# Two-layer attention and gate stack on one core: odd heads' probabilities of the last two items and the last gate products on VectorE, spare products in the drain, negated mean ahead of the power

## What is computed

```
x = x + attn_a(layernorm(x))   # softmax attention with rotary terms
x = x + ffn(layernorm(x))
x = x + attn_b(layernorm(x))   # causal sparsemax attention
x = x + ffn(layernorm(x))

attn_*: 16 heads of 8 columns, scores 256 x 256 for each head
sparsemax(z) = max(z - tau, 0), tau from the sorted, summed scores
ffn(x) = (silu(x @ wg.T) * (x @ wu.T)) @ wd.T, hidden width 384
```

## Time and profile before

| | before |
|---|---|
| median of 3 runs | 621.91 us (621.61 to 622.36) |
| the profiled execution | 621.83 us |
| its span (first to last instruction on the core) | 618.7 us |
| TensorE, VectorE, ScalarE, GpSimd busy | 94%, 78%, 68%, 63% |
| end of the last product, of the last VectorE addition | 613.7 us, 614.1 us |

### The profile page before, as it was taken

How to read it: one execution, slowest core, us unless ns; L and a number is a source line. 1 busy time by engine, 2 the same in 40 slices (tenths; PEclk the granted TensorE clock), 3 DMA queues, 4 the chain that set the end, 5 groups by cost and what they waited for, 6 DMA issues and landing times.

```text
span 618.7 us, 19166 instructions
## 1 busy us (share of the span) xinstructions
PE 582.1 (94%) x6716; PEld 451.5 (73%) x6716; DVE 484.8 (78%) x1421; ACT 422.8 (68%) x1057; POOL 389.7 (63%) x824
## 2 busy tenths in 40 slices
PE   5897999999999999999999999999999999999984
PEld 4674556767777776777677888778888888888663
DVE  2298778888888888987787888887888888899332
ACT  1113667778777777778787777767777877777762
POOL 4745446677776667777666766676666666653341
PEclk9999999999999999999999999989999999999997
DMA  3587577765666655545444445432655544440000
GB/s 93 137 238 183 127 165 173 165 168 149 149 154 149 151 134 136 144 119 136 132 124 131 122 124 116 117 82 76 138 115 124 120 108 123 117 124 21 12 10 21
DMA packets 74439, 76.23 MB, mean 123 GB/s; under 512 B 10276, under 2 KB 68836, under 8 KB 69732
## 3 DMA queue, kind: packets, MB, share of 16 engines
q1 hardware_dynamic: 74340, 74.97, 48.7%
HBM read 46.86 MB, written 23.33 MB: 113 GB/s over the span
## 4 chain that ended last, share of the span: by engine, by line
PE 67%; DVE 15%; issue 5%; ACT 4%; POOL 4%; DMA 3%; SPq 0%; POOLq 0%; ACTq 0%; DVEq 0%
PE banks L1501 14%; PE banks L1455 9%; PE banks L1479 8%; PE banks L1432 7%; PE banks L1371 6%; DVE top L1102 4%; PE banks L1423 3%; DVE top L1101 3%; PE banks L1458 3%; PE banks L1403 2%; PE banks L1424 2%; DVE neg_shift L1096 2%; ACT probs_t L1291 2%; PE banks L1482 2%; PE banks L1381 2%
## 5 line engine op out<-in xcount | busy, mean ns | idle before, releaser
L1291 ACT ACTIVATE probs_t<-banks 128x512 f32<-128x512 f32 (+1 forms) x512 | 266.9, 551 | 79.2 <-PE banks L1479 51.6
L1096 DVE TENSOR_REDUCE neg_shift<-banks 128x2 f32<-128x512 f32 x256 | 166.1, 681 | 42.4 <-PE banks L1455 41.2
L1501 PE MATMUL banks<-probs_t,v_ext 128*32 128x256 f32 (+1 forms) x2048 | 118.9, 361 | 0.1
L1455 PE MATMUL banks<-k_stack,q_stack 72*128 72x256 bf16 x512 | 99.8, 276 | 8.4 <-DVE neg_shift L1096 2.9
L1102 DVE MAX8 top<-banks 128x8 f32<-128x256 f32 x256 | 105.6, 413 | 0.0
L1479 PE MATMUL banks<-q_stack,k_stack 75*128 75x256 bf16 x512 | 98.8, 274 | 0.2
L987 POOL TENSOR_TENSOR hidden<-up_tanh,gate_half 128x256 f32<-128x256 f32 x96 | 70.0, 732 | 43.6 <-DVE up_tanh L1142 38.2
L1101 DVE MAX8 top<-banks 128x8 f32<-128x128 f32 x256 | 74.1, 290 | 26.3 <-PE banks L1464 25.3
L1501 PEld LDWEIGHTS banks<-probs_t,v_ext 128*32 128x32 f32 x2048 | 55.9, 110 | 39.1 <-issue 14.6
L1455 PEld LDWEIGHTS banks<-k_stack,q_stack 72*128 72x128 bf16 x512 | 41.3, 98 | 46.9 <-DVE neg_shift L1096 33.1
L1458 PE MATMUL banks<-k_stack,q_stack 128*128 128x128 bf16 x256 | 56.6, 221 | 6.2 <-DVE top L1102 4.6
(11 more groups left out here) (108 smaller groups left out, 1387.2 us busy)
## 6 DMA issues: line engine op xcount, KB each, us to landing
q_stack<-q_image SPq DMA_DIRECT2D x96, 192.0 KB
k_stack<-k_image SPq DMA_DIRECT2D x96, 192.0 KB
q_image<-qk_parts SPq DMA_DIRECT2D x32, 192.0 KB, 2.3
k_image<-qk_parts SPq DMA_DIRECT2D x32, 192.0 KB, 2.1
q_image<-qk_parts SPq DMA_DIRECT2D x32, 128.0 KB, 2.2
o_image<-out_t SPq DMA_DIRECT2D x32, 128.0 KB, 1.9
out_compact<-o_image SPq DMA_DIRECT2D x32, 64.0 KB
rdenominators<-r_image SPq DMA_DIRECT2D x16, 128.0 KB, 2.5
```

Source lines behind the costliest of these rows:

```text
L1096: dve.tensor_reduce(m.nm[:, n % STACKS, h, :], scores.rearrange("p (q k) -> p q k", q=TT), AX.X, ALU.max, negate=True).then_inc(reduced, 1)
L1291: act.activation(m.pt[:, (n * Q + g) % GROUPS, i, 0:size], shifted_banks[:, j % 2, 0:size], ACT.Exp if is_soft(n) else ACT.Relu, scale=SCA ...
L1455: ins = pe.matmul(scores[:, qt * T:(qt + 1) * T], qs[0:STACK, h, qt * P:(qt + 1) * P], ks[0:STACK, h, :], start=True, stop=True)
L1501: ins = pe.matmul(out_bank[32 * i:32 * i + 32, at + skip:at + T], v_windows(v, kt)[:, Q * g + i, :], m.pt[:, (n * Q + g) % GROUPS, i, kt * ...
```

## The change

- `probs` on ScalarE leaves out the odd heads of items 30 and 31 (`SPLIT = ITEMS - 2`); VectorE makes them with a `tensor_scalar` maximum with 0 at the end of the same step (`odd_probs`), under a semaphore of its own, `odd_probs_ready`. `pass2` and `pv` wait for the one, the other or both.
- The three products `hidden` of item 31 go from GpSimd to VectorE, each right behind its `up_times` (`last_hidden`).
- TensorE issues spare products in the drain: 30 at step 551 behind the projection of item 31, 6 at step 558 behind its turn, 14 at step 568 behind its gates (`TAIL_SPARE`).
- `rstd_a` and `rstd_f` negate the mean ahead of the power instead of behind it, and wait for the mean first; this is so in all 32 items.

```diff
+SPLIT = ITEMS - 2
+TAIL_SPARE = {16 * (ITEMS - 1) + 55: 30, 16 * (ITEMS - 1) + 62: 6, 16 * (ITEMS - 1) + 72: 14}
+def act_probs(n, j):
+    return n * H + j + 1 if n < SPLIT else SPLIT * H + (n - SPLIT) * (H // 2) + j // 2 + 1
+def dve_probs(n, j):
+    return (n - SPLIT) * (H // 2) + (j + 1) // 2
...
             def rstd_f(n):
+                pool.wait_ge(f_var, n * TT + TT)
+                pool.tensor_scalar(m.f_neg[:, :], m.f_mv[:, :, 0], -1.0, None, ALU.mult).then_inc(f_rstd, 1)
                 pool.wait_ge(f_eps, n + 1)
                 wait(pool, f_xhat, n * TT)
                 pool.tensor_tensor(m.f_rstd[:, :], m.f_ve[:, :], m.neghalf[:, 0:TT], ALU.pow).then_inc(f_rstd, 1)
-                pool.tensor_scalar(m.f_neg[:, :], m.f_mv[:, :, 0], -1.0, None, ALU.mult).then_inc(f_rstd, 1)
                 pool.wait_ge(f_rstd, 2 * n + 2)
...
-                    if (n := due(step, f"hid{c}")) is not None:
+                    if (n := due(step, f"hid{c}")) is not None and n < ITEMS - 1:
                         hidden(n, c)
...
+            def odd_probs(n, j):
+                g, i = divmod(j, Q)
+                wait(dve, pv_done, n * Q + g + 1 - GROUPS)
+                dve.wait_ge(shifted_ready, n * H + j + 1)
+                dve.tensor_scalar(m.pt[:, (n * Q + g) % GROUPS, i, 0:T + P], shifted_banks[:, j % 2, 0:T + P], 0.0, None,
+                                  ALU.max).then_inc(odd_probs_ready, 1)
+
+            def last_hidden(n, c):
+                wait_freed(dve, f"gu{c}", n)
+                wait_filled(dve, "down", n - 1)
+                k = (n * NC_H + c) % 3
+                dve.tensor_tensor(m.hid[:, c, :], m.t1[:, k, :], m.g05[:, k, :], ALU.mult).then_inc(hid_ready, 1)
...
+                        if n == ITEMS - 1:
+                            last_hidden(n, c)
...
+                n, j = divmod(step - AT["pass2"], H)
+                if SPLIT <= n < ITEMS and j % 2 == 1:
+                    odd_probs(n, j)
...
-                wait(pe, probs_ready, n * H + (j - 1))
+                if n >= SPLIT and j % 2 == 1:
+                    wait(pe, odd_probs_ready, dve_probs(n, j - 2))
+                if n < SPLIT or j % 2 == 0 or (n == SPLIT and j == 1):
+                    wait(pe, probs_ready, act_probs(n, j - 2) if j > 1 else act_probs(n - 1, H - 2 + j))
...
+                for i in range(TAIL_SPARE.get(step, 0)):
+                    spare()
```

More of the change, by code:

```diff
@@ L698, in main_phase @@
     probs_ready = sem("probs_ready")
+    odd_probs_ready = sem("odd_probs_ready")
     pv_done = sem("pv_done")
@@ L908, in rstd_a @@
             def rstd_a(n):
+                pool.wait_ge(a_var, n * TT + TT)
+                pool.tensor_scalar(m.a_neg[:, :], m.a_mv[:, :, 0], -1.0, None, ALU.mult).then_inc(a_rstd, 1)
                 pool.wait_ge(a_eps, n + 1)
@@ L911, in rstd_a @@
                 pool.tensor_tensor(m.a_rstd[:, :], m.a_ve[:, :], m.neghalf[:, 0:TT], ALU.pow).then_inc(a_rstd, 1)
-                pool.tensor_scalar(m.a_neg[:, :], m.a_mv[:, :, 0], -1.0, None, ALU.mult).then_inc(a_rstd, 1)
                 pool.wait_ge(a_rstd, 2 * n + 2)
@@ L1339, in _ @@
                 n, j = divmod(step - AT["pass2"], H)
-                if 0 <= n < ITEMS:
+                if 0 <= n < ITEMS and (n < SPLIT or j % 2 == 0):
                     probs(n, j)
@@ L1492, in pv @@
             def pv(n, g):
-                pe.wait_ge(probs_ready, n * H + Q * g + Q)
+                pe.wait_ge(probs_ready, act_probs(n, Q * g + Q - 1))
+                if n >= SPLIT:
+                    pe.wait_ge(odd_probs_ready, dve_probs(n, Q * g + Q - 1))
                 if g == 0:
```

## The result

| | before | after |
|---|---|---|
| median, 20 runs each | 622.11 us (618.18 to 623.90) | **617.53 us** (612.97 to 622.62) |
| ratio | | 0.9929, 95% interval 0.9908 to 0.9950 |
| the profiled execution | 621.83 us | 617.57 us |
| its span | 618.7 us | 615.8 us |
| time outside its span | 3.1 us | 1.8 us |

The change is faster by 0.7%. The forecast was 620.6 us with a range of 619.5 to 621.8, so it had the sign right as its likelier side (0.47) and the size too small by 3.1 us. Five single executions of 700 us and more, three of them of the kernel before, are in the medians and left out of the means of spans and clocks.

What follows compares the result with a forecast made beforehand. TensorE, busy in 94% of the span, waits for ScalarE's probabilities in late pass 2; a chain of single operations sets the drain. 621.83 - 1.03 - 0.20 = 620.6 us, range 619.5 to 621.8.

Steps and rivals of the forecast that it cites:

- From there all is as before: Behind the last `down`, forecast at 611.05 against 612.08: everything that follows was taken as unchanged.
- Sum inside the span: Whole kernel: -1.03 us from odd heads, spares and last products together, and -0.20 us at the start.
- Part 1: Pass 2 of items 30 and 31, odd heads on VectorE: -0.15 us, ends -1.5 and +0.3.
- about 2: Sign to look for: TensorE's waits in pass 2 still total about 2 us, for VectorE as well as ScalarE.
- Rival (a): Pass 2: ScalarE is the true bound, so moving heads removes 2.0 us in place of 0.15; 618.8 us, 12%.
- Part 2: Drain: spares keep the clock full; they cost 0.2 us net up to the turn, later gates come sooner.
- worth 1.0 us: Drain: at full clock the second and third gates are out at 609.0 against 610.0 before.
- Rival (b): Drain or pass 2: clock falls anyway or maxima take 0.68 us; up to 0.8 us more, 621.4 us, 23%.
- Rival (c): Drain: the thirty spares become the path, costing time if ending after 603.3; at half clock 623.9 us, 7%.
- Part 3: Drain: last products take 0.42 us on VectorE against 0.73 on GpSimd; last `down` at 611.05 against 612.08.
- Part 4: Start: negating the mean earlier brings item 0's normalised rows 0.20 us sooner; worth nothing in item 31's drain.

Runs made afterwards that it cites:

- p1: Kernel before plus three never-executed memsets in VectorE's skipped second path: 619.64 us, ratio 0.9996, 1.80 us outside the span.
- p3: Kernel before plus 40 never-executed memsets in VectorE's skipped second path: 621.52 us, ratio 1.0012, 1.81 us outside the span.
- p4: Kernel before plus 120 never-executed memsets in VectorE's skipped second path: 618.00 us, ratio 0.9976, 1.85 us outside the span.
- p2: Control: kernel before plus three never-executed copies in ScalarE's skipped second path: 622.29 us, ratio 1.0034, 3.41 us outside the span.
- e8: The changed kernel with all heads on ScalarE again: 617.70 us, ratio 0.9958 against the kernel before.
- e4: Kernel before with only the last three hidden products moved to VectorE: 619.15 us, ratio 0.9947.
- e5: The changed kernel without its fifty spare products in the drain: 615.47 us, ratio 0.9923 against the kernel before.
- c1: The changed kernel measured again, nothing altered, beside the kernel before: 618.38 us, ratio 0.9964.
- e2: Kernel before with only the fifty spare products in the drain: 620.61 us, ratio 0.9986.
- c2: Kernel before with only 22 spare TensorE products added at step 31: 618.84 us, ratio 0.9964.
- e1: Kernel before with only the negated mean ahead of the power: 620.60 us, ratio 0.9995.

## Why the prediction was right or wrong

**The step that failed is "From there all is as before".** It carried the 3.1 us outside the span over unchanged, as a term at nothing. Outside is 3.42 us in the runs of before and 1.79 in those of the change; p1, p3 and p4 against p2 show that a longer VectorE program does this even if nothing of the addition is executed. Half of the gain over all runs is this (1.6 of 3.1 us), and no row of the span could have shown it. What could have been seen is that the profile leaves 3.1 us without a name, and a term without a name has bounds too. Of the 3.1 us by which the forecast missed the median, 1.6 are this step. Another 0.6 is its base: one profiled execution of 621.83 us, where before's runs in the four series have a mean of 621.27. 0.2 is the size inside the span, and 0.6 is that the median of 20 runs, 617.53, lies below the mean of all 32 runs of the change, 618.14.

**Sum inside the span: right in size over runs, too small for the profiled pair.** Forecast -1.23, measured -1.5 ± 0.5 over the runs and -2.90 between the two profiled executions. The rest of the pair is what the two happened to draw: the stretch near 409 us, seen in two of 17 traces (before and p2), and the stores behind the last addition, which take 3.61 to 3.93 us in 14 of 17 traces and 4.3 or more in three, of which before is one. That the sum over the runs comes out is in part luck: its drain term was taken from before's trace, whose last stretch is the shortest of eight. The last stretch is 41.72 and 41.76 us in the two traces of the change, against 43.09 in the mean of the eight.

**Part 1 (-0.15): nothing.** The maxima take 0.54 to 0.56 us as worked out:

```profile
571.12 0.54 DVE L1127 TENSOR_SCALAR probs_t<-banks 128x384 f32<-128x384 f32 x1
...
573.08 0.55 DVE L1127 TENSOR_SCALAR probs_t<-banks 128x384 f32<-128x384 f32 x1
...
574.12 0.42 DVE L1174 SCALAR_TENSOR_TENSOR up_tanh<-gate_tanh,banks 128x256 f32<-128x256 f32 x1 [0.49 <-ACT gate_half L1354]
574.46 0.55 DVE L1127 TENSOR_SCALAR probs_t<-banks 128x384 f32<-128x384 f32 x1
```

The Trainium skill, "VectorE: DVE Perf Modes", section "The TRN2 errata — SBUF-src ops pay a fixed extra latency per instruction", by which the forecast estimated 0.53 us, agrees. Head 3 (573.08) stands behind `tau`, head 5 (574.46) behind `up_times` which waits for a gate, as foreseen. But the waits stay at 2.6 us, where "about 2" was said, and the gates of item 30 start 0.09 us later in relation to the same instruction. e8 puts it at +0.07, inside the ends of -1.5 and +0.3.

**Rival (a), ScalarE bounds pass 2: refuted.** ScalarE's load in the two stretches fell from 22.45 to 16.85 us and TensorE did not get through sooner. Busy without gaps is not the same as bounding: where nothing else stands between, the next head waits for the round trip of its bank, on whichever engine. Heads 11 and 13 of item 30, as in the earlier trace rows, now with VectorE between them:

```profile
579.26 0.23 PE L1522 MATMUL banks<-q_stack,k_stack 128*128 128x128 bf16 x1
...
579.74 0.56 DVE L1127 TENSOR_SCALAR probs_t<-banks 128x384 f32<-128x384 f32 x1 [0.33 <-PE banks L1528]
...
580.35 0.23 PE L1522 MATMUL banks<-q_stack,k_stack 128*128 128x128 bf16 x1 [0.53 <-DVE probs_t L1127]
```

That is 1.09 us, with ScalarE 1.01. The forecast had them equal, because VectorE was to start 0.06 us sooner behind the product. It starts 0.48 us behind the head's first product, ScalarE 0.46.

**Part 2, spares: each step as forecast, but the comparison was with the wrong alternative.** From the projection, forecast and measured: `down` of item 30 at +3.80 and +3.79, the turn at +5.22 and +5.13, the first gate at +6.55 and +6.43, all gates out at +8.69 and +8.39. The flag's product stands 0.2 us off the end of the first gate's pieces (606.23 plus 0.12, then 606.55), as said. The clock stayed full. But "worth 1.0 us" was priced against a drain at half the clock, and with the products on VectorE the clock may not fall at all (e4, e5), so that in e5's place the thirty spares are a pure loss of 0.67 us. Rival (b) did not come either: the clock stayed full to the last `down` in all seven traces with spares. Rival (c) had named the point from which they decide, spares that end after 603.3. The projection is 0.97 us earlier in after than the forecast had it (600.31), so their end at 603.13 is 604.10 in the forecast's frame: past that point by 0.8 us, as the sum had it with 604.11, and near what e5 gives back.

**Part 3, products on VectorE: right in its steps.**

```profile
607.76 0.42 DVE L1134 TENSOR_TENSOR hidden<-up_tanh,gate_half 128x256 f32<-128x256 f32 x1
...
609.44 0.42 DVE L1134 TENSOR_TENSOR hidden<-up_tanh,gate_half 128x256 f32<-128x256 f32 x1
...
611.56 0.42 DVE L1180 TENSOR_TENSOR x<-banks,x 128x256 f32<-128x256 f32 x1 [1.70 <-PE banks L1469]
```

They take 0.42 us each, and the last `down` starts 10.58 us behind the projection against 10.74 forecast. Its place in the span, 609.92 against 610.85, differs by 0.77 of what came before the drain and by 0.16 of the drain. The last stretch as a whole shrank by 0.94 us in after and 0.90 in c1, forecast 1.03. The products' own share of it is some 0.2 us, as the times from the last gate to the last `down` in e2 and after show; the rest is the clock that the spares kept.

**Part 4, negated mean: right at the start, and hidden in the drain as forecast.**

```profile
3.94 0.22 POOL L927 TENSOR_SCALAR a_neg_mean<-a_mean_var 128x2 f32<-128x2 f32 x1 [1.10 <-DVE a_mean_var L1078]
4.13 0.71 POOL L930 TENSOR_TENSOR a_rstd<-a_var_eps,neghalf 128x2 f32<-128x2 f32 x1
4.92 0.19 POOL L932 TENSOR_TENSOR a_norm_bias<-a_neg_mean,a_rstd 128x2 f32<-128x2 f32 x1
```

The product that needed it starts at 4.92, before at 5.14. The first scores came 0.54 us sooner in after, but 0.32 sooner in c2 as well, which does not have this part: their time hangs on when the stacks of k land, and 0.2 us is within that. In the drain it takes 0.19 us out where the turn waits for ScalarE (e1, e5), and nothing behind thirty spares, as the forecast said. e1 as a whole is 0.9995 of before.

**Range.** Terms of 0.1 us were worked out with care beside two things of over 1 us that were taken as fixed: the time outside the span and the luck of one profiled execution. Both were measurable only over many runs; the three runs shown ahead (621.61 to 622.36) lie within 0.8 us, the 20 of the result within 5.7.

## What to carry to other kernels

Before an edit worth 0.2% is judged, set device time against span for every run, and clock against span: a gain that appears outside the span is not the edit's idea at work, and a median of runs with different clocks compares luck. Parts that cure the same wait don't add, so cost a filler against the kernel with the other parts in, not against the one before. And look at the stretches at half the clock early in the program: covering the idle time ahead of one of them brought 2.8 ± 0.8 us, and all four parts of this change 1.5 ± 0.5 inside the span.

## What the hardware showed that I had not expected

- Three instructions that VectorE never executes take 1.6 us off what lies outside the span (3.42 to 1.80), and none of it is seen inside (617.93 ± 0.77 against 617.58 ± 0.49 us); three on ScalarE do nothing (3.41). In the traces the 1.6 us are a pause between the third and the fourth update of semaphore 2 behind the last instruction.
- Twelve of 14 traces have a stretch at half the clock behind TensorE's idle time at step 32; with 22 spare products there, none of three has it. Before has 0.94 in the window 50 to 80 us, c2 1.00, and c2's span is 2.8 us shorter over the runs (the stretch near 30 us is gone with it, so not all of this is its own). The Trainium skill, "TensorE: Matmul & The Clock Gate", Part 1, puts the cost of the clock's ramp below 1% of a typical kernel's span. No run here takes the ramp at the start by itself; what the two later stretches cost stays below that mark too (2.8 of 618 us is 0.45%), but for a tuned kernel it is more than most edits bring.
- Idle time alone does not decide it: ahead of the last `down` e5 was idle for 2.04 us, and in c2 TensorE stood for 2.07 us ahead of the first scores, and the clock was full behind both.
